# Coefficient pass spread away from the last pair, two down buffers and four sign slots, context stage with takes and squares in front of the combinations

## The chip, the core and the metric

The kernel runs on one core of a Trainium2 chip. The metric is the device time of one execution in microseconds (us). TensorE (PE) multiplies matrices from SBUF into PSUM, VectorE (DVE), ScalarE (ACT) and GpSimd (POOL) work elementwise, and the queues of SyncE (SP) and POOL issue the DMA transfers, which all run on the same 16 DMA engines. The engines run side by side; each works through its own instructions in order and waits on semaphores.

## The reference

It is one decoder layer over 2 x 512 tokens of width 1024, in three parts, each with a residual and a layer norm in front:

```
x = x + mamba2 block with its own gated MLP (gate, up, down; inner width 3584)      # first feed-forward
q1 = fake_quant(layernorm(x));  q2 = fake_quant(ctx)      # ctx 2 x 1024 x 1024
x = x + q1 @ q2                                           # context stage
W = base + mean(|w - base|) * sign(w - base)   for w1, w2, w3   # coefficient and signs
x = x + (silu(n @ W1.T) * (n @ W3.T)) @ W2.T,  n = layernorm(x)  # second feed-forward
```

`mean(|w - base|)` is one number for each of the three matrices, over 3584 x 1024 weights, so all weights must be read before the first formed weight can be written.

## The kernel before

**The two feed-forwards** (m = 0 and m = 1) are computed with a scheme of seven products in place of eight for a 2 x 2 split of each operand (`t` = 0 to 6), and each fp32 factor is split into a high and a low part, so that a product is three matmuls per tile. A *step* is 12 matmuls of 128x512 (L912 for gate and up, `product`; L937 for the down projection, `down_step`). The gate and up part has 14 *pairs* (p = 0 to 13) of 14 steps, or *turns* (7 products, each for gate, x = 0, and up, x = 1); the down part has 98 steps (2 halves `sc`, 7 products, 7 inner tiles k). Weights go through a ring of seven slots: ACT writes the high part (`weight_hi`, L1155), DVE the sum where there is one and the low part (`weight_sum`, `weight_lo` L1568), both five to six steps ahead of TensorE. The results of the gate and up steps leave PSUM by `gate_up_out` on DVE (L1654, L1664, L1674, L1682), `gate_out` (L1218 the last) and `psum_copy` on ACT. ACT and DVE go through one list of steps each and do at turn i of a pair what tables put there.

**The coefficient pass** runs beside the first feed-forward. Its 84 blocks of 128x1024 stand at the turns of `CF_TURNS` from pair 1 on: SP loads both blocks (`load_coeff`, two of 512 KB, L466) when the block two before has been used, DVE subtracts (`coeff_diff`, L1704), ACT writes the sign as int8 and sums the absolute values (`coeff_abs`), POOL stores the signs. From pair 6 on, two context tiles per pair are quantized too (`quantize`, L1708 to L1712, and `q2_sum`, at turns 5 and 9). Before: 7 blocks in each of pairs 1 to 6, 6 in each later one, 6 in pair 13.

**The last pair** of either feed-forward is where SP starts to load the down part: after turns 1, 3, ..., 13 it issues eight loads of 256 KB (`first_down_loads`, L487), 56 in all, into combination tiles that TensorE has done with, then four x quarters of 1 MB (`load_x_quarter`). SP's queue is one list; a wait in it holds up all that stands behind.

**The second feed-forward** forms its weights as it goes: `form_weight` (DVE, L1728) adds sign x coefficient to the base weights in place. Signs come through `sign_in` (2 slots), down weights through one buffer `down_formed`: SP loads (`load_down`, L597), DVE forms, POOL stores to HBM (`store_down`, L677); the next load waits for that store. The 28 down tiles are formed two in each of pairs 1 to 12 (turns 2 and 10) and four in pair 13 (turns 0, 3, 6, 9).

**The context stage** stands between. For batch b: centre, squares, variance sums on TensorE (`ctx_var`, L962), root (ACT L1399/L1400, DVE `ctx_rsqrt` L2019 to L2022), rounding of q1 (DVE and ACT in turn, `ctx_round`, ACT L1409 writes q1), products (`ctx_first`: four output tiles together, k outermost, L968, and the row sums L981; then `second_tile` one by one), a correction (`minus_mean`, L973), and `ctx_take` (DVE L2054), which adds the product to x. `ctx_columns` (ACT L1415) adds a column term to x in front of the takes, from `column_sums` (TensorE L954). `second_mean` (L986 and DVE L2047) keeps the mean of the new x. Then squares of the new x, their variance sums (three groups: rsqrt 3, 4, 5), and the combinations `comb(1, t)` (DVE L1609 makes, ACT L1201 high part, L1618/L1615 low part) that feed the second feed-forward. `prefill` fills the ring for its first steps.

## Time and profile before

| | us |
|---|---|
| three runs, median (lowest, highest) | 2228.65 (2228.29, 2229.97) |
| the profiled execution: its own time | 2227.82 |
| its span in the profile | 2226.0 |
| PE busy in the span | 2125.9 (96%) |
| DVE busy | 1667.7 (75%) |
| ACT busy | 1050.2 (47%) |

All times further down are counted from the start of the span. Up to about 363 us runs the mamba2 part, up to 455 us its output projection, from about 490 to 1308 the first feed-forward, to about 1391 the context stage, then the second feed-forward to 2221. A busy PE is not a PE at its peak: matmuls overlap, and the granted clock (PEclk, as a share of full speed) falls after TensorE has been idle.

### The profile page before, as it was taken

The page shows a single profiled execution, that of the slowest core. Times are in us where ns is not written, and L with a number is a line of the kernel's source. Part 1 is how long each engine was busy: PE and PEld are TensorE (multiplying, and loading weights), DVE is VectorE, ACT ScalarE, POOL GpSimd, SP SyncE. Part 2 cuts the span into 40 slices and gives each one's busy share as a digit, 9 for nine tenths or more (in the row PEclk, how much of TensorE's full clock was granted, in tenths as well). Part 3 has the DMA queues.
Part 4 walks back from the last instruction along what each step waited for, and adds up shares of the span by engine and source line. Part 5 has one row for each costly group of instructions (what it writes and reads, how often), then busy time and mean ns, then how long its engine had stood idle before and what let it go on. Part 6 is the DMA issues. An engine that isn't in the chain of part 4 may idle for free.

```text
span 2226.0 us, 26830 instructions
## 1 busy us (share of the span) xinstructions
PE 2125.9 (96%) x9266; PEld 1688.9 (76%) x9266; DVE 1667.7 (75%) x2498; ACT 1050.2 (47%) x1710; POOL 175.5 (8%) x287
## 2 busy tenths in 40 slices
PE   7999998969999999998999998899999999899999
PEld 4777776847888888886888853688888888788887
DVE  7776556478777888886979888977777677498785
ACT  4333234236777777775444456433333333344442
POOL 0000010000111111110000000200000000000000
PEclk9999999979999999999999998899999999999999
DMA  3151002516888989889160032644444443754201
GB/s 119 38 198 38 20 28 97 144 19 218 293 308 300 328 314 309 315 304 396 62 212 1 1 133 86 165 148 168 148 168 150 173 147 142 265 206 162 99 19 57
DMA packets 132958, 361.61 MB, mean 162 GB/s; under 512 B 16288, under 2 KB 27168, under 8 KB 129184
## 3 DMA queue, kind: packets, MB, share of 16 engines
q1 hardware_dynamic: 108912, 279.78, 36.5%
q0 software_dynamic: 23920, 80.23, 10.5%
q8 instruction: 70, 1.15, 0.2%
q14 instruction: 56, 0.46, 0.1%
HBM read 279.73 MB, written 84.41 MB: 164 GB/s over the span
## 4 chain that ended last, share of the span: by engine, by line
PE 81%; DVE 11%; ACT 3%; DMA 2%; issue 2%; SPq 1%; DVEq 0%; ACTq 0%
PE pair L912 41%; PE pair L937 24%; PE pair L717 9%; DVE conv_out L1867 1%; DVE comb_lo L1618 1%; PE pair L968 1%; SPq L487 1%; DMA down_formed<-b_dn 1%; PE pair L855 1%; PE pair L856 1%; PE pair L830 1%; DVE ring_lo L1568 1%; PE pair L837 1%; DMA wd_spill<-down_formed 1%; PE pair L753 1%
## 5 line engine op out<-in xcount | busy, mean ns | idle before, releaser
L912 PE MATMUL pair<-comb_hi,ring_hi 128*128 128x512 f32 x1568 | 618.4, 394 | 47.1 <-DVE comb_lo L1615 11.1
L912 PE MATMUL pair<-comb_lo,ring_hi 128*128 128x512 f32 x1568 | 616.0, 393 | 0.0
L912 PE MATMUL pair<-comb_hi,ring_lo 128*128 128x512 f32 x1568 | 615.4, 393 | 0.0
L912 PEld LDWEIGHTS pair<-comb_hi,ring_hi 128*128 128x128 f32 x1568 | 298.1, 190 | 117.0 <-issue 36.0
L937 PE MATMUL pair<-inner_ring_a,ring_hi 128*128 128x512 f32 x1120 | 346.4, 390 | 2.2 <-DVE second_copy_a L1674 2.2
L912 PEld LDWEIGHTS pair<-comb_hi,ring_lo 128*128 128x128 f32 x1568 | 297.9, 190 | 62.9
L912 PEld LDWEIGHTS pair<-comb_lo,ring_hi 128*128 128x128 f32 x1568 | 298.0, 190 | 61.9 <-issue 0.2
L937 PEld LDWEIGHTS pair<-inner_ring_a,ring_hi 128*128 128x128 f32 x1120 | 210.8, 188 | 46.5 <-issue 2.6
L937 PE MATMUL pair<-inner_ring_a,ring_lo 128*128 128x512 f32 x560 | 218.5, 390 | 0.0
L1155 ACT ACTIVATE ring_hi<-ring_sum 128x512 fp32r<-128x512 f32 x168 | 106.0, 631 | 157.7 <-DVE ring_sum L1555 155.8
L717 PE MATMUL pair<-act_hi,weights_hi 128*128 128x512 f32 x416 | 138.6, 415 | 12.0 <-DVE act_lo L1511 7.6
L937 PE MATMUL pair<-inner_ring_b,ring_hi 128*128 128x512 f32 x448 | 138.4, 390 | 0.0
L1568 DVE TENSOR_TENSOR ring_lo<-raw_a,ring_hi 128x512 fp32r<-128x512 f32 x140 | 95.4, 685 | 50.2 <-ACT ring_hi L1155 50.1
L717 PE MATMUL pair<-act_lo,weights_hi 128*128 128x512 f32 x416 | 129.7, 393 | 0.0
L717 PE MATMUL pair<-act_hi,weights_lo 128*128 128x512 f32 x416 | 129.3, 392 | 0.0
L1256 ACT ACTIVATE sign_out<-pair 128x1024 int8<-128x1024 f32 x84 | 85.9, 1022 | 86.7 <-DVE pair L1704 86.7
L937 PEld LDWEIGHTS pair<-inner_ring_a,ring_lo 128*128 128x128 f32 x560 | 105.5, 188 | 22.0
L1568 DVE TENSOR_TENSOR ring_lo<-ring_sum,ring_hi 128x512 fp32r<-128x512 f32 x168 | 114.9, 684 | 1.3
L1704 DVE TENSOR_TENSOR pair<-coeff_in 128x1024 f32<-128x1024 f32 x84 | 103.0, 1226 | 16.2 <-DMA coeff_in<-b_dn 14.5
L717 PEld LDWEIGHTS pair<-act_hi,weights_hi 128*128 128x128 f32 x416 | 78.0, 191 | 35.9 <-issue 20.7
L937 PEld LDWEIGHTS pair<-inner_ring_b,ring_hi 128*128 128x128 f32 x448 | 84.1, 188 | 17.9 <-issue 0.5
L717 PEld LDWEIGHTS pair<-act_lo,weights_hi 128*128 128x128 f32 x416 | 78.9, 190 | 17.0
(334 smaller groups left out, 3189.6 us busy)
## 6 DMA issues: line engine op xcount, KB each, us to landing
coeff_in<-f_gu SPq DMA_DIRECT2D x56, 512.0 KB, 5.1
coeff_in<-b_gu SPq DMA_DIRECT2D x56, 512.0 KB, 6.9
weights_raw<-w_mamba SPq DMA_DIRECT2D x28, 512.0 KB, 3.2
raw_a<-w_gu SPq DMA_DIRECT2D x28, 512.0 KB, 7.2
raw_a<-w_gu SPq DMA_DIRECT2D x56, 256.0 KB, 6.2
u_spill<-gate_a POOLq DMA_DIRECT2D x56, 256.0 KB, 6.1
coeff_in<-f_dn SPq DMA_DIRECT2D x28, 512.0 KB, 4.8
coeff_in<-b_dn SPq DMA_DIRECT2D x28, 512.0 KB, 6.8
```

The source lines that it names most:

```text
L487: sp.dma_start(d_tile(m, kind, k), src).then_inc(s_ld[group // 2][k], 16)
L717: ins = pe.matmul(out[:, half * 512:(half + 1) * 512], w[:, wi, wcol * P:(wcol + 1) * P], a[:, half * 512:(half + 1) * 512], start=first a ...
L753: return pe.matmul(out[:, HALF[b]], ones[:, :], src[:, HALF[b]], start=first, stop=last)
L830: ins = pe.matmul(ps[1][:, g * 512:(g + 1) * 512], ones[:, :], cs_rhs[:, g * HPG:(g + 1) * HPG, :], start=True, stop=False, skip_group_che ...
L837: pe.matmul(ps[2][:, g * 512:(g + 1) * 512], bx_cur[:, 2 + g, :], xbc[:, 4 + g * HPG:4 + (g + 1) * HPG, bass.ds(b * SEQ + c * P, P)], star ...
L855: pe.matmul(ps[2][:, h * P:(h + 1) * P], x_dt[:, h, :], att[:, h, :], start=True, stop=False)
L912: ins = pe.matmul(out, wt[:, slot, col], a, start=t in (0, 1, 3) and kk == 0 and n == 0, stop=kk == KH - 1 and n == 2, skip_group_check=True)
L937: ins = pe.matmul(out, wt[:, slot, col], a, start=t in (0, 1, 3) and k == 0 and n == 0, stop=k == SC_PAIRS - 1 and n == 2, skip_group_chec ...
L1155: act.activation(WRH[:, slot, :], src, ACT.Copy).then_inc(s_whi, 1)
L1256: act.activation(sign_out[:, c % 2, :], dif_ps[:, :], ACT.Sign).then_inc(s_sign, 1)
L1568: TT(WRL[:, slot, :], src, WRH[:, slot, :].bitcast(F32), ALU.subtract).then_inc(s_wlo, 1)
L1704: TT(dif_ps[:, :], dif[:, c % 2, 0, :], dif[:, c % 2, 1, :], ALU.subtract).then_inc(s_cd, 1)
```

## The change

1. `CF_TURNS`: 7 blocks in pairs 1 to 9, 6 in pairs 10 to 12, 3 in pair 13 (turns 1, 3, 6). The number of blocks is the same, 84.
2. `stage_d` becomes two buffers, used in turn by down tile; `load_down(j)` waits for the store of tile j - 2. `sign_in` becomes four slots; the signs are loaded four forms ahead. In the context stage the signs of forms 4 to 7 are loaded behind both loads of `raw_odd`.
3. Context stage: the column sums of batch 1 go behind the first products of batch 0; ACT takes the root of batch 1 between two halves of the column additions; `ctx_first` leaves its fourth output tile out up to k = `late` and makes it up behind a wait, so that batch 1's products wait for the fourth take and not for the fifth and `second_mean(0)`; both `second_mean` stand behind the last variance sums; on DVE all takes and squares of batch 1 come in front of `comb(1, 0)`.
4. Semaphores are merged (`var_ready` into `norm_var_ready`, the dt and cs ones), with the counts to match.

Core of the diff:

```diff
-CF_TURNS = {p: ((1, 3, 5, 7, 9, 11, 13) if p <= 6 else (1, 3, 6, 8, 11, 13)) for p in range(1, PAIRS)}
-CF_TURNS[PAIRS - 1] = (1, 3, 6, 7, 8, 11)
+CF_TURNS = {p: (1, 3, 5, 7, 9, 11, 13) if p <= 9 else (1, 3, 6, 8, 11, 13) for p in range(1, PAIRS)}
+CF_TURNS[PAIRS - 1] = (1, 3, 6)
...
-    stage_d = at("down_formed", 144 * KB, [P, BLK], F32)
-    sign_in = at("sign_in", 192 * KB, [P, 2, BLK], I8)
+    stage_d = (at("down_formed_a", 144 * KB, [P, BLK], F32), at("down_formed_b", 194 * KB, [P, BLK], F32))
+    sign_ab, sign_cd = at("sign_in_ab", 192 * KB, [P, 2, BLK], I8), at("sign_in_cd", 198 * KB, [P, 2, BLK], I8)
+    sign_in = (sign_ab[:, 0, :], sign_ab[:, 1, :], sign_cd[:, 0, :], sign_cd[:, 1, :])
...
         def load_down(j):
-            if j >= 1:
-                sp.wait_ge(s_do_st, 16 * j)
-            sp.dma_start(stage_d[:, :], b_dn[j]).then_inc(s_sd, 16)
+            if j >= 2:
+                sp.wait_ge(s_do_st[j % 2], 16 * (j // 2))
+            sp.dma_start(stage_d[j % 2][:, :], b_dn[j]).then_inc(s_sd[j % 2], 16)
...
         spill_x2(0)
-        load_sign(4)
-        load_sign(5)
         spill_x2(1)
         load_second(1, 0)
         load_second(1, 1)
+        for f in range(4, 8):
+            load_sign(f)
...
-        def ctx_first(b, banks, rows):
+        def ctx_first(b, banks, rows, late, start):
             for k in range(KT):
                 pe.wait_ge(s_q1, b * KT + k + 1)
-                for o in range(KH):
+                for o in range(KH if k > late else KH - 1):
                     ctx_mm(b, o, k, banks[o])
...
+                if k == late:
+                    start()
+                    for kk in range(k + 1):
+                        ctx_mm(b, KH - 1, kk, banks[KH - 1])
...
-        second_mean(0, bank(5))
-        pe.wait_ge(s_xt, 5)
-        pe.wait_ge(s_m2, 1)
-        ctx_first(1, [bank(n) for n in (1, 2, 6, 4)], bank(5))
+        pe.wait_ge(s_xt, 4)
+        ctx_first(1, [bank(n) for n in (1, 2, 6, 4)], bank(5), 2, lambda: pe.wait_ge(s_xt, 5))
...
-        ctx_columns(0, range(KT))
+        ctx_columns(0, range(KH))
         ctx_root(3, bank(7))
+        ctx_columns(0, range(KH, KT))
...
-        ctx_take(1, range(2), (1, 2))
-        prefill(1, range(2, RING))
-        ctx_take(1, range(2, KH), (6, 4))
+        ctx_take(1, range(KH), (1, 2, 6, 4))
+        ctx_take(1, range(KH, 6), (3, 0))
+        prefill(1, range(2, 4))
+        ctx_take(1, range(6, KT), (1, 2))
+        square_pairs(5, x_square, range(3))
         comb(1, 0)
-        ctx_take(1, range(KH, 6), (3, 0))
-        square_pairs(5, x_square, range(2))
-        ctx_take(1, range(6, KT), (1, 2))
-        square_pairs(5, x_square, range(2, 3))
-        second_mean(1)
-        for kk in range(KH):
-            make(1, "b21", kk)
+        second_mean(0, bank(6))
+        second_mean(1, bank(3))
         ctx_rsqrt(5, bank(7))
-        comb(1, 1, made=True)
+        comb(1, 1)
+        prefill(1, range(4, RING))
```

SP's queue in the last pair of the first feed-forward, before (`coeff_in` are the two blocks of the coefficient pass, `comb_*_f_0t` the down quarters of tile t, `ctx_in` a context tile):

```order
L487 DMA comb_lo_f_00_109<-u_spill 128x512
L466 DMA coeff_in<-f_dn 128x1024
L466 DMA coeff_in<-b_dn 128x1024
L487 DMA comb_lo_f_01_110<-w_dn 128x512
...
L487 DMA comb_lo_f_02_111<-u_spill 128x512
L466 DMA coeff_in<-f_dn 128x1024
L466 DMA coeff_in<-b_dn 128x1024
L466 DMA coeff_in<-f_dn 128x1024
L466 DMA coeff_in<-b_dn 128x1024
L487 DMA comb_lo_f_03_112<-w_dn 128x512 x4
```

and now, in the same place:

```order
L467 DMA coeff_in<-f_dn 128x1024
L467 DMA coeff_in<-b_dn 128x1024
L488 DMA comb_hi_f_00_81<-w_dn 128x512
...
L488 DMA comb_lo_f_00_109<-u_spill 128x512
L488 DMA comb_lo_f_01_110<-w_dn 128x512
...
L488 DMA comb_lo_f_02_111<-u_spill 128x512
L488 DMA comb_lo_f_03_112<-w_dn 128x512 x4
```

Three pairs of block loads are gone from between the down quarters; the last one stands in front of them.

DVE in the context stage, from the last root but one to the combinations for t = 2, before (`centred<-pair` are takes, `x_mid<-x_mid` sums of squares, `comb_hi_f_16` and `comb_lo_f_16` the makes of t = 0 and 1):

```order
L2054 SCALAR_TENSOR_TENSOR centred<-pair,quant_columns,centred 128x512 x2
L1609 TENSOR_TENSOR comb_hi_f_16_94<-centred,scratch_c_155 128x512 x2
...
L2054 SCALAR_TENSOR_TENSOR centred<-pair,quant_columns,centred 128x512 x2
L2013 TENSOR_TENSOR x_mid<-x_mid 128x512
L2047 SCALAR_TENSOR_TENSOR scratch_c_155<-pair,quant_columns,scratch_c_155 128x512
L1609 TENSOR_TENSOR comb_lo_f_16_122<-centred,scratch_c_155 128x512 x4
L2019 SCALAR_TENSOR_TENSOR scratch_c_155<-scratch_c_155 128x512
L2020 SCALAR_TENSOR_TENSOR scratch_c_155<-pair,scratch_c_155 128x512
L2022 SCALAR_TENSOR_TENSOR scratch_c_155<-scratch_c_155 128x512
L1618 TENSOR_TENSOR comb_lo_103<-comb_lo_f_16_122,comb_hi_75 128x512 x4
L1609 TENSOR_TENSOR comb_lo_f_15_121<-centred,scratch_c_155 128x512 x4
```

and now:

```order
L2060 SCALAR_TENSOR_TENSOR centred<-pair,quant_columns,centred 128x512 x2
L2019 TENSOR_TENSOR x_mid<-x_mid 128x512 x3
L1615 TENSOR_TENSOR comb_hi_f_16_94<-centred,scratch_c_157 128x512 x2
...
L2053 SCALAR_TENSOR_TENSOR scratch_c_157<-pair,quant_columns,scratch_c_157 128x512 x2
L2025 SCALAR_TENSOR_TENSOR scratch_c_157<-scratch_c_157 128x512
L2026 SCALAR_TENSOR_TENSOR scratch_c_157<-pair,scratch_c_157 128x512
L2028 SCALAR_TENSOR_TENSOR scratch_c_157<-scratch_c_157 128x512
L1615 TENSOR_TENSOR comb_lo_f_16_122<-centred,scratch_c_157 128x512 x2
...
L1574 TENSOR_TENSOR ring_lo<-raw_even,ring_hi 128x512 x3
L1615 TENSOR_TENSOR comb_lo_f_15_121<-centred,scratch_c_157 128x512 x4
```

The last takes and all three sums of squares stand in front of the first combination, the root between the two combinations, and three fills of the ring behind both.

## Rows read from the trace of the kernel before

**Rows 1.** The page, part 1: busy time, share, instructions per engine.

```profile
PE 2125.9 (96%) x9266; PEld 1688.9 (76%) x9266; DVE 1667.7 (75%) x2498; ACT 1050.2 (47%) x1710; POOL 175.5 (8%) x287
```

**Rows 2.** TensorE's waits: line, releaser, us in total, times, longest.

```profile
PE pair L912 <- DVE first_copy_b L1664: 8.4, 1, 8.4
PE pair L912 <- DVE gate_a L1664: 7.2, 1, 7.2
PE pair L962 <- DVE x_mid L2013: 6.2, 1, 6.2
```

**Rows 3.** Chain of waits, second feed-forward's last pair: start us, us, what.

```profile
1923.76 5.38 DMA wd_spill<-down_formed
...
1934.23 7.55 DMA wd_spill<-down_formed
1941.80 5.34 DMA down_formed<-b_dn
...
1954.11 266.60 PE pair L937 x1176
```

**Rows 4.** DVE timeline, both last pairs: start, us, line, operation [idle before, releaser].

```profile
993.50 0.69 DVE L1654 TENSOR_TENSOR gate_a<-first_copy_a,pair 128x512 f32<-128x512 f32 x1 [1.46 <-PE pair L912]
...
1023.12 1.23 DVE L1704 TENSOR_TENSOR pair<-coeff_in 128x1024 f32<-128x1024 f32 x1 [14.50 <-DMA coeff_in<-b_dn]
...
1913.71 0.69 DVE L1654 TENSOR_TENSOR gate_b<-first_copy_b,pair 128x512 f32<-128x512 f32 x1 [1.46 <-PE pair L912]
```

**Rows 5.** Chain of waits, first feed-forward's last pair and end.

```profile
1011.97 11.12 DMA coeff_in<-b_dn
...
1034.53 257.56 PE pair L937 x1128
...
1307.81 3.19 PE pair L954 x128
```

**Rows 6.** Windows: stretch, us, busy per engine, granted clock, DMA share, GB/s.

```profile
718.70:756.80 38.10, 37.67 (x167) 30.90 (x166) 30.50 (x45) 29.11 (x49) 6.97 (x13) 1.00 0.94 326
756.80:794.90 38.10, 38.10 (x170) 31.55 (x169) 31.94 (x46) 27.75 (x47) 6.95 (x12) 1.00 0.91 323
996.00:1057.00 61.00, 51.54 (x213) 41.76 (x212) 42.05 (x65) 33.84 (x58) 5.92 (x11) 0.92 1.05 396
1911.00:1958.00 47.00, 38.58 (x162) 31.47 (x161) 23.66 (x36) 15.17 (x28) 3.53 (x7) 0.89 0.95 344
```

**Rows 7.** TensorE timeline, context stage.

```profile
1311.96 5.14 PE L1008 MATMUL pair<-x_mid,ones_over_dm 128*128 128x512 f32 x8
...
1343.59 1.88 PE L986 MATMUL pair<-x_mid_rounded,x_mid 4*128 4x512 f32 x4
1348.79 1.87 PE L968 MATMUL pair<-q,q 128*128 128x512 bf16 x4 [3.32 <-DVE centred L2054]
...
1360.76 3.70 PE L962 MATMUL pair<-x_mid,ones_over_dm 128*128 128x512 f32 x8
```

**Rows 8.** DVE timeline, context stage: the last three roots, first make for t = 2.

```profile
1334.57 0.69 DVE L2019 SCALAR_TENSOR_TENSOR scratch_c<-scratch_c 128x512 f32<-128x512 f32 x1 [3.64 <-ACT scratch_c L1400]
...
1365.88 0.69 DVE L2019 SCALAR_TENSOR_TENSOR scratch_c<-scratch_c 128x512 f32<-128x512 f32 x1 [3.72 <-ACT scratch_c L1400]
...
1393.05 0.69 DVE L2019 SCALAR_TENSOR_TENSOR scratch_c<-scratch_c 128x512 f32<-128x512 f32 x1 [3.52 <-ACT scratch_c L1400]
...
1397.64 3.09 DVE L1609 TENSOR_TENSOR comb_lo_f<-centred,scratch_c 128x512 f32<-128x512 f32 x5
```

**Rows 9.** TensorE's waits in the stretch 740 to 760 us.

```profile
PE pair L912 <- ACT gate_a L1218: 0.4, 1, 0.4
```

**Rows 10.** ACT timeline, context stage.

```profile
1328.31 4.99 ACT L1415 ACTIVATE centred<-centred,column_terms 128x512 f32<-128x512 f32 x8
1333.21 0.66 ACT L1399 ACTIVATE scratch_c<-pair,quant_columns 128x512 f32<-128x512 f32 x1
...
1350.01 0.71 ACT L1409 ACTIVATE q<-scratch_c,quant_columns 128x512 bf16<-128x512 f32 x1
```

More of the change, by code:

```diff
@@ L357, in build @@
     s_sq, s_sqd = sem("square_ready"), sem("square_used")
-    s_t, s_root = sem("var_ready"), sem("root_ready")
     s_a, s_ah, s_act = sem("act_value"), sem("act_hi_ready"), sem("act_ready")
@@ L389, in build @@
     s_q2 = [sem(f"q2_in{b}") for b in range(BATCH)]
-    s_sgn = [sem(f"sign_in{i}") for i in range(2)]
+    s_sgn = [sem(f"sign_in{i}") for i in range(4)]
     s_sign, s_form = sem("sign_ready"), sem("second_formed")
     s_so = [sem(f"sign_stored{i}") for i in range(2)]
-    s_sd, s_do_st = sem("down_raw_in"), sem("down_formed_stored")
+    s_sd = [sem(f"down_raw_in{i}") for i in range(2)]
+    s_do_st = [sem(f"down_formed_stored{i}") for i in range(2)]
     s_x1, s_u2, s_c5 = sem("first_copied"), sem("second_copied"), sem("fifth_copied")
@@ L601, in _ @@
         load_second(0, 0)
-        load_sign(0)
-        load_sign(1)
+        for f in range(4):
+            load_sign(f)
         load_second(0, 1)
-        load_sign(2)
-        load_sign(3)
         load_down(0)
+        load_down(1)
         def spill_x2(b):
@@ L625, in _ @@
                     f = FORM_AT[14 * p + turn - 1]
-                    if f + 2 < N_FORM:
-                        load_sign(f + 2)
+                    if f + 4 < N_FORM:
+                        load_sign(f + 4)
                 if 14 * p + turn - 2 in FORM_AT:
                     what = FORM_WHAT[FORM_AT[14 * p + turn - 2]]
-                    if what[0] == "d" and what[1] + 1 < ITILES:
-                        load_down(what[1] + 1)
+                    if what[0] == "d" and what[1] + 2 < ITILES:
+                        load_down(what[1] + 2)
                 if p == PAIRS - 1:
@@ L813, in _ @@
         pe.matmul(ps[2][:, 256:320], tri, a_all[:, :, :], start=True, stop=True)
[L814 removed]
+        pe.matmul(ps[2][:, 320:384], ones[:, :], a_all[:, :, :], start=True, stop=True).then_inc(s_dtm, 1)
         conv_pair(CONV_TILES // 2 - 1)
@@ L997, in _ @@
         feed_forward(W_END[0] - 2, W_END[0])
-        for b in range(BATCH):
-            column_sums(b, bank(3))
+        column_sums(0, bank(3))
         pe.wait_ge(s_xs, 2)
@@ L1012, in _ @@
         pe.wait_ge(s_m1, 1)
-        pe.wait_ge(s_ht, 3)
+        pe.wait_ge(s_ht, 2 + BATCH + 1)
         pe.wait_ge(s_q2[0], 16 * KT)
-        pe.wait_ge(s_do, 4 * 13 + KH)
-        ctx_first(0, [bank(n) for n in (0, 1, 2, 6)], bank(5))
+        ctx_first(0, [bank(n) for n in (0, 1, 2, 6)], bank(5), 0, lambda: pe.wait_ge(s_do, 4 * 13 + KH))
+        column_sums(1, bank(3))
         ctx_var(bank(7), x_square, range(KH), KT + KH, (), 0)
@@ L1064, in _ @@
         minus_mean(1, bank(2))
-        second_mean(1, bank(5))
-        pe.wait_ge(s_ht, 5)
+        pe.wait_ge(s_ht, 4 + BATCH + 1)
         ctx_var(bank(7), x_square, range(3), KT + 3 * KH, (6, 7), 5 * KT)
-        pe.wait_ge(s_xt, 2 * KT)
-        feed_forward(BASE_G[1], BASE_G[1] + 1)
+        second_mean(0, bank(6))
+        second_mean(1, bank(3))
+        feed_forward(BASE_G[1], BASE_G[1] + 4)
         pe.wait_ge(s_m2, 2)
-        feed_forward(BASE_G[1] + 1, W_END[1])
+        feed_forward(BASE_G[1] + 4, W_END[1])
     @blk.scalar
@@ L1188, in inner_hi @@
                         act.wait_ge(s_so[i], 16 * (CF_BLOCKS // 2))
-                if m == 1 and slot == 4:
-                    act.wait_ge(s_do_st, 16 * ITILES)
+                if m == 1 and slot >= 4:
+                    for i in range(2):
+                        act.wait_ge(s_do_st[i], 16 * (ITILES // 2))
                 if m == 1 and slot >= 5:
@@ L1447, in _ @@
         ctx_root(4, bank(7))
-        for w in range(2, RING):
+        ctx_columns(1, range(KH, KT))
+        for w in range(2, 4):
             weight_hi(BASE_G[1] + w)
-        ctx_columns(1, range(KH, KT))
-        taken_squares(1, range(KH))
+        taken_squares(1, range(KT))
         comb_hi(1, 0)
-        taken_squares(1, range(KH, KT))
+        ctx_root(5, bank(7))
         comb_hi(1, 1)
-        ctx_root(5, bank(7))
+        for w in range(4, RING):
+            weight_hi(BASE_G[1] + w)
         feed_forward(1)
@@ L1716, in form_tile @@
             if what[0] == "d":
-                return stage_d[:, :]
+                return stage_d[what[1] % 2][:, :]
             return rawF[what[1] % 2][:, what[2], 2 * what[3]:2 * what[3] + 2, :].rearrange("p a h -> p (a h)")
@@ L2041, in rows_lo, with second_mean @@
             STT(mean_rows(b, 1), bank(5)[0:4, :], -1.0 / DM, mean_rows(b, 0).bitcast(F32), ALU.mult, ALU.subtract).then_inc(s_rlo, 1)
-        def second_mean(b):
+        def second_mean(b, out):
             kept = scr_c(7)[:, HALF[b]]
@@ L2046, in second_mean @@
             dve.wait_ge(s_csumd, b + 2)
-            STT(kept, bank(5), S12, kept, ALU.mult, ALU.add).then_inc(s_m2, 1)
+            STT(kept, out, S12, kept, ALU.mult, ALU.add).then_inc(s_m2, 1)
         def ctx_take(b, tiles, banks):
@@ L2079, in _ @@
         ctx_take(0, range(6, KT), (3, 0))
-        second_mean(0)
         ctx_round(1, range(6, KT + 1))
```

47 lines of the change are left out of this document (25 added, 22 removed).

## The prediction

> **What bounds the kernel now.** I read the page's busy times first: TensorE is busy for 2125.9 of 2226.0 us [rows 1]. The rest of the time, and the time that its matmuls lose to a lower granted clock, are all that this change can reach. The list of TensorE's waits says where it stands still: 8.4 us for `first_copy_b`, 7.2 us for `gate_a`, 6.2 us for the sums of squares of L2013 [rows 2]. The waits of the first two blocks of the kernel (L717, L753) are longer in sum but lie outside the change.
>
> Step length: 1176 matmuls take 266.60 us [rows 3], so a step of 12 matmuls takes 2.72 us and a pair of 14 steps 38.08 us.
>
> *First feed-forward, last pair.* The DVE row of L1654 at 993.50 [rows 4] comes at the end of step 2, so this pair began at 993.50 - 3 x 2.72 = 985.3 and its 14 steps should end at 1023.4. The down steps (L937) begin at 1034.53 [rows 5], 11.1 us late. Their first 1128 matmuls then take 257.56 us where 94 steps need 255.7, 1.9 us more, the slow restart after the idle time. Together 13.0 us. The cause is the DVE row at 1023.12: it stood 14.5 us for block 82 of the coefficient pass, whose load was issued at 1011.97 and took 11.12 us [rows 4, 5]. SP had issued it behind the down quarters, and the DMA engines were full: 396 GB/s from 996 to 1057 [rows 6].
>
> *Second feed-forward, last pair.* L1654 at 1913.71 [rows 4] puts the pair's start at 1905.55 and its end at 1943.6; the down steps begin at 1954.11, 10.5 us late [rows 3]. The chain of waits goes store, load, form, store, load through the one buffer `down_formed`: 5.38 us of store, 7.55 us of store, 5.34 us of load [rows 3]. The steps at turns 3, 6 and 9 come every 8.16 us, and one round of store and load takes 12.9 us (7.55 + 5.34).
>
> *Context stage.* TensorE waits 3.3 us before the second batch's products start at 1348.79 [rows 7], and 6.2 us before the last group of variance sums [rows 2]. Behind that the limit is VectorE: the combinations for t = 2 of the second feed-forward start at 1397.64 [rows 8], and TensorE waits for them and for the ring several times before it has caught up.
>
> **The change part by part.** The sum is made against the profiled execution's own 2227.82 us; the median of the runs is 0.8 us above.
>
> 1. *Last pair of the first feed-forward: -13.0 us.* Blocks per pair fall from 6 to 3; only block 83 is still loaded in it, in front of the down quarters. Of the four block loads that stood in this queue one is left, 3.1 MB (3 x 2 x 0.52) less. Is there another wait right behind? SP issues 8 quarters (2.1 MB) after each second step. From 996 on: 1.2 MB of backlog (my estimate from the 3.1 MB issued in the 6 us before), 12.6 MB of quarters, 0.5 of context, 4.2 MB of x quarters, 2 MB of stores: 20.5 MB, or 52 us at 396 GB/s, to 1048. In that order the set of turn 5, with the inner tiles of k = 1 to 4, is in by about 1012 (first needed 1012.5 by ACT, five steps ahead of TensorE); the set of turn 11 by 1030 (needed by VectorE from 1026.1, by TensorE from 1042); the first x quarter by 1038.6 (needed at 1042.4). So everything is in before TensorE wants it, with the 13 us of the seven-slot ring to spare. Bounds: 7.9 (only the 3.1 MB leave, at 396 GB/s) to 13.0.
>
> 2. *Pairs 7 to 9: +1.3 us.* Each gets one block more (DVE 1.23 us, ACT 2.1 us) beside its two context tiles. Pair 6 already has just this load: DMA share 0.94 and TensorE busy 37.67 of 38.10 us [rows 6], with one wait of 0.4 us for ACT's `gate_a` [rows 9]. Pair 7, with one block less, has none (38.10 busy). 3 x 0.43 = 1.3. Bounds 0 to 4 (if a late pair hands its lateness on).
>
> 3. *Last pair of the second feed-forward: -10.5 us.* With two buffers the load of tile 26 goes out where that of tile 25 went (about 1915.7), is in at about 1922 and is wanted at turn 6, 1905.55 + 16.3 + 1 = 1923. Tile 27 waits for the store of tile 25 (formed 1915.5, stored by 1922 to 1924), and is in by about 1928 to 1930, wanted at turn 9, 1931. The last store ends near 1941, when ACT wants inner slot 4, five steps before TensorE. VectorE may stand for up to 3 us at turn 11 and after, because the same bytes now have to come in 10 us less; the ring covers it. Bounds: 5 to 10.5. The four sign slots change nothing by themselves: before, no wait of TensorE lies in pairs 1 to 12. In pair 0 the signs of forms 4 to 7 now stand in SP's queue behind both `raw_odd` loads (2.1 MB), which the forms need anyway.
>
> 4. *Context stage: -6.5 us.* (a) Half of the column sums (3.19 us together, [rows 5]) goes behind the first products: these start 1.6 us earlier, less what the clock takes (L1008 needs 5.14 us behind the column sums, L962 with as many matmuls 3.70, [rows 7]). (b) ACT takes 4 of the 8 column additions (4.99 us, [rows 10]) behind the root of L1399, so the root starts when the variance sums end, 1331 to 1333.3, not at 1333.21 [rows 10]; I take 1332, 1.2 us earlier. The chain behind (L2019 at 1334.57, takes, rounding) moves by as much. (c) The second batch's products no longer wait for `second_mean(0)` (0.7 us on DVE, 1.9 us on PE) nor for the fifth take, but for the fourth, with the fourth bank caught up at k = 2. TensorE had no other work from 1343.6 on than L986 [rows 7], so the products start there or soon after; the pace is then the rounding: the column for k = 4 was written from 1350.01 on [rows 10] and is ready 1.9 us earlier (1.2 from (b), 0.7 from `second_mean(0)`), 1348.9; TensorE is at 1349.1 by then, and four steps of 1.28 us and the rest of the fourth end at 1354.2 where it was 1360.8 [rows 7]: 6.6 us. Lower end of the gain 5, upper 7.5 (root at 1331.3). (d) From the variance sums to the root L1399 and L2019 (1365.88 before, [rows 8]) the order is as before, so VectorE goes on 6.3 us earlier. (e) Behind it the same operations stand in another order: eight takes, three sums of squares, two combinations of eight operations, two mean updates (one more than before), the root, nine prefill operations. Before, from 1368.1 (1365.88 and three operations) to 1397.64 it took 29.6 us, of them 3.5 us idle in front of L2019 at 1393.05 [rows 8]. Now the squares are ready in front of the first combination, so the root is computed beside it; but each combination alternates with ACT at its own pace (1 us lost each, as the first one does now), and the takes of tiles 4 to 7 wait for TensorE (0.5 us at each of two places). I come to 29.2 us: 0.4 us gained. 6.3 + 0.4 = 6.7, taken as 6.5. (f) Behind 1397.64 VectorE works without a gap until TensorE has caught up, before and after, with the same instructions, so what it gains in front is what the kernel gains. Bounds 0 (see rival B) to 8.
>
> 5. *Merged semaphores* (`var_ready` into `norm_var_ready` and so on): counts only, 0.
>
> Sum: -13.0 + 1.3 - 10.5 - 6.5 = -28.7; 2227.8 - 28.7 = 2199.1, by the runs' median 2200.
>
> On the DMA rate: the row shows 396 GB/s over 61 us, reads and stores together [rows 6].
> The Trainium skill (DMA: Bandwidth & Descriptors, Specifications and Where 436 GB/s comes from) gives an HBM limit of about 358 GB/s per core when both cores of a pair stream, and 425 measured for one core alone; by the 358 the 20.5 MB of part 1 would take 57 us and the first x quarter would come at about 1043, just when it is wanted. The trace of this one-core program is above the 358, so I stay with 396.
>
> **Rivals.**
>
> A. *The DMA engines are the true limit of both last pairs.* Then removing DVE's wait only moves it to the quarter loads. For it: the share of 1.05 over 61 us [rows 6], and that the same quarters must now arrive 10 to 13 us sooner. Against it: before, TensorE has no wait in either down phase, and the ring is five steps ahead. Price: the first stage gets back 3.1 MB / 0.396 = 7.9 us, the second what 344 instead of 396 GB/s left over 47 us [rows 6], 47 x (1 - 344/396) = 6.2. Sum: -7.9 + 1.3 - 6.2 - 6.5 = -19.3: 2209. The same time would come if the waits fell away and most of the clock's loss stayed.
>
> B. *The context stage gives nothing.* If the part behind L2019 is longer by what the part before is shorter (two combinations in a row, each in step with ACT, and two mean updates on VectorE in front of the last root), or the start of the products at the fourth take runs into the rounding, 6.5 us go: 2206.5. Speaks for it: VectorE has hardly an idle stretch there but those in front of L2019. Against: the 6.6 us of (c) lie in front of a VectorE that idles 3.7 us before 1365.88 [rows 8], at the end of a chain that starts with TensorE.
>
> C. *Slower: pairs 7 to 9 tip over.* The mechanism is that of 1023 in three more places: a block's load comes late, VectorE stands with it in order, and `gate_a` and the ring behind it are late for TensorE. One such wait cost 13 us; three of them are 39 us against the 30 that the other parts give: 2227.8 + 39 - 30 = 2237. It decides once the blocks cost more than 10 us per pair, that is, when a load lands over 10 us late. Against it: pair 6 with the same bytes loses 0.43 us.
>
> D. *The change does not do what it says in the second feed-forward:* tile 27 still waits for the store of tile 25, that store took 7.55 us at its worst, and the load comes behind two sets of quarters; if it lands at 1938 instead of 1930, VectorE stands 7 us and TensorE perhaps 2: 2202. Small, inside the range.
>
> **How the numbers follow.** My forecast with its small variants (and D) 0.68, A 0.15, B 0.10, C 0.03, and 0.04 for something not seen here that eats nearly all of it (0.01 still faster, 0.02 the same, 0.01 slower). The likeliest is 2200. A and B together would be 2216, too unlikely to be held. The range goes from 2195 (no cost in pairs 7 to 9, 8 us in the context stage, a little more clock) to 2212 (A with a little of B). About 0.2% (4.5 us) is what a measurement can tell from no change. So faster 0.94, same 0.02, slower 0.04.
>
> **What would show it right or wrong.** In the profile after: no wait of VectorE over 1 us on `coeff_in` and on `down_formed`; L937 begins 38.1 us after the last pair's start in both halves (within 1 us); three more waits of about 0.4 us on `gate_a` L1218 at the ends of pairs 7 to 9; the second batch's products start without a wait near the end of the first batch's and end 6 to 7 us earlier, counted from the end of the first feed-forward; the first combination for t = 2 starts 6 to 7 us earlier by the same count. I am wrong if L937 shows gaps in its first fourteen steps with DMA behind them (A), if the distance from L2019 to the t = 2 combinations has grown (B), or if pairs 7 to 9 are longer than 39 us (C).

## The result and the profile after

| | before | after |
|---|---|---|
| median of the runs (lowest, highest), us | 2228.47 (2228.20, 2229.97), 4 runs | 2204.30 (2200.11, 2204.72), 4 runs |
| ratio, 95% interval | | 0.9886 (0.9869 to 0.9903) |
| profiled execution: own time, span | 2227.82, 2226.0 | 2204.26, 2202.4 |

The change takes 24 us off; 2200 was predicted. The line numbers have moved by a few: L912 is now L913, L937 L938, L962 L963, L1218 L1222, L1704 L1710.

First TensorE's busy time, part 1 of the page, which answers to [rows 1], and the list of its waits (line, releaser, us in total, times, longest):

```profile
PE 2123.8 (96%) x9262; PEld 1687.1 (77%) x9266; DVE 1668.0 (76%) x2498; ACT 1051.5 (48%) x1710; POOL 174.8 (8%) x287
```

```profile
PE pair L913 <- DVE comb_lo L1621: 12.4, 6, 6.0
...
PE pair L913 <- ACT gate_a L1222: 2.6, 5, 0.8
PE pair L963 <- DVE x_mid L2019: 1.8, 1, 1.8
```

The waits of 8.4 us for `first_copy_b` and 7.2 for `gate_a` L1664 [rows 2] are gone, and the 6.2 us for the sums of squares are 1.8. What has grown is small: there are five waits for `gate_a` L1222 (2.6 us) where the trace of before has two (0.9 us, one of them in [rows 9]). The three more stand at the ends of pairs 7 to 9 and are the price of the blocks there. The six waits for `comb_lo` L1621 at the starts of the feed-forwards are 12.4 us in place of 11.1, the longest 6.0 in place of 3.3.

The chain of waits of the changed kernel, start, us, what:

```profile
530.09 209.74 PE pair L913 x924
...
876.08 152.56 PE pair L913 x672
1028.64 255.69 PE pair L938 x1128
...
1930.54 266.57 PE pair L938 x1176
```

In both halves the products of the last pair run straight into the down steps. The 1128 matmuls take 255.69 us, which is 94 of the steps of 2.72 us, so nothing is lost to a lower clock, where [rows 5] had 257.56. The two down phases begin at 1028.64 and 1930.54, where [rows 5] and [rows 3] have 1034.53 and 1954.11.

To see where the 23.6 us of span went, I cut both profiled executions at the first and the last matmul of each kind (views of the product line and of the down line: first and last start):

| stretch | before | after | difference |
|---|---|---|---|
| start to the first product of the first feed-forward | 471.7 | 474.4 | +2.7 |
| first feed-forward, products and down | 835.7 | 825.3 | -10.4 |
| context stage and the second feed-forward's products | 646.6 | 630.7 | -15.9 |
| second down phase and end | 272.0 | 272.0 | 0.0 |

The first row is not the change's; e4 and e10 deal with it. How far such stretches differ between executions of the same code stands in the last section.

### The profile page after: what moved, and what is told of

Its sections match the earlier page's. It is cut to its first block, busy times and chain, and to the rows that moved or that the text cites. A ratio compares the mean times of both kernels' runs of the same rounds, so it can differ in the third digit from the quotient of the medians.

```text
span 2202.4 us, 26828 instructions
## 1 busy us (share of the span) xinstructions
PE 2123.8 (96%) x9262; PEld 1687.1 (77%) x9266; DVE 1668.0 (76%) x2498; ACT 1051.5 (48%) x1710; POOL 174.8 (8%) x287
## 4 chain that ended last, share of the span: by engine, by line
PE 82%; DVE 12%; ACT 3%; issue 2%; DMA 1%; DVEq 0%; SPq 0%; ACTq 0%
PE pair L913 41%; PE pair L938 24%; PE pair L718 9%; DVE conv_out L1873 1%; PE pair L969 1%; DVE comb_lo L1624 1%; DVE ring_lo L1574 1%; PE pair L831 1%; DVE pair L1710 1%; PE pair L856 1%; PE pair L857 1%; PE pair L838 1%; PE pair L754 1%; PE pair L860 1%; PE pair L963 1%
## 5 line engine op out<-in xcount | busy, mean ns | idle before, releaser
L913 PE MATMUL pair<-comb_hi,ring_hi 128*128 128x512 f32 x1568 | 618.4, 394 | 34.7 <-DVE comb_lo L1621 12.4
L913 PE MATMUL pair<-comb_hi,ring_lo 128*128 128x512 f32 x1568 | 615.6, 393 | 0.0
L913 PE MATMUL pair<-comb_lo,ring_hi 128*128 128x512 f32 x1568 | 615.6, 393 | 0.0
L913 PEld LDWEIGHTS pair<-comb_hi,ring_hi 128*128 128x128 f32 x1568 | 297.8, 190 | 106.8 <-issue 22.9
L913 PEld LDWEIGHTS pair<-comb_hi,ring_lo 128*128 128x128 f32 x1568 | 297.7, 190 | 62.5
L913 PEld LDWEIGHTS pair<-comb_lo,ring_hi 128*128 128x128 f32 x1568 | 298.2, 190 | 61.5
L938 PE MATMUL pair<-inner_ring_a,ring_hi 128*128 128x512 f32 x1120 | 344.9, 389 | 0.0
L938 PEld LDWEIGHTS pair<-inner_ring_a,ring_hi 128*128 128x128 f32 x1120 | 210.1, 188 | 43.6
L938 PE MATMUL pair<-inner_ring_a,ring_lo 128*128 128x512 f32 x560 | 217.9, 389 | 0.0
L938 PE MATMUL pair<-inner_ring_b,ring_hi 128*128 128x512 f32 x448 | 138.3, 390 | 0.0
L938 PEld LDWEIGHTS pair<-inner_ring_a,ring_lo 128*128 128x128 f32 x560 | 105.1, 188 | 21.9
L1710 DVE TENSOR_TENSOR pair<-coeff_in 128x1024 f32<-128x1024 f32 x84 | 103.0, 1227 | 0.3 <-DMA coeff_in<-b_gu 0.3
L938 PEld LDWEIGHTS pair<-inner_ring_b,ring_hi 128*128 128x128 f32 x448 | 84.1, 188 | 17.9 <-issue 0.5
```

What stands on the lines that cost most here:

```text
L913: ins = pe.matmul(out, wt[:, slot, col], a, start=t in (0, 1, 3) and kk == 0 and n == 0, stop=kk == KH - 1 and n == 2, skip_group_check=True)
L938: ins = pe.matmul(out, wt[:, slot, col], a, start=t in (0, 1, 3) and k == 0 and n == 0, stop=k == SC_PAIRS - 1 and n == 2, skip_group_chec ...
L1710: TT(dif_ps[:, :], dif[:, c % 2, 0, :], dif[:, c % 2, 1, :], ALU.subtract).then_inc(s_cd, 1)
```

## The experiments

All medians are of four or more runs; the kernel before gave 2224.2 to 2234.8 in 50 runs beside them, and I take a median of five as good to about 1.5 us. Where less matters I go by the stretches of the traces. Line numbers of the variants differ by a few from those of the changed kernel.

### e1: the block table alone

```diff
-CF_TURNS = {p: ((1, 3, 5, 7, 9, 11, 13) if p <= 6 else ...
-CF_TURNS[PAIRS - 1] = (1, 3, 6, 7, 8, 11)
+CF_TURNS = {p: (1, 3, 5, 7, 9, 11, 13) if p <= 9 else ...
+CF_TURNS[PAIRS - 1] = (1, 3, 6)
```

> Only CF_TURNS changed (7 blocks in pairs 1 to 9, 6 in 10 to 12, 3 in pair 13). Theory 1 (the parts act by themselves, as the two traces read): the last pair gives 13.0 us back, pairs 7 to 9 cost 2.6 us (their lengths in the trace after are 38.8, 39.2 and 38.8 us for 38.1), net -10.4: 2218.1 us. Theory 2 (the 2.8 us that the changed kernel is later before its first feed-forward belong to this part): 2220.9. The prediction's own numbers: -13.0 + 1.3 = -11.7, 2216.8. Rival A (DMA engines are the limit): about -5, 2223.

Measured 2220.25 us (2218.38 to 2221.09) against 2228.1; ratio 0.9963 (0.9949 to 0.9977), so -7.9 us. In its trace the first feed-forward takes 825.5 us, 10.2 less than in the trace of before, as theory 1 says. But the kernel before does not always lose so much there: in e2, e4 and e8, which have its block table, the same stretch takes 833.9, 834.1 and 833.6 us (in e3, which has it too, 835.3). So the table, gain in the last pair less cost in pairs 7 to 9, is worth 8.1 to 10.4 us by the executions that one compares. With the 2.6 us that pairs 7 to 9 cost, the last pair gives back 10.7 to 13.0 us, and the 13.0 that the prediction read from one trace are the upper end. Rival A's 5 us stands at the very edge of the interval (0.9977) and above all five runs; the trace speaks against it with its 10.2 us.

### e2: buffers and sign slots; e8: the sign slots alone; e4: the merged semaphores alone

e2 has `stage_d` and `sign_in` as in the change, without the other parts; e8 is e2 with

```diff
-    stage_d = (at("down_formed_a", ...), at("down_formed_b", ...))
+    stage_d = (at("down_formed", 144 * KB, [P, BLK], F32),) * 2
...
-            if j >= 2:
-                sp.wait_ge(s_do_st[j % 2], 16 * (j // 2))
+            if j >= 1:
+                sp.wait_ge(s_do_st[(j - 1) % 2], 16 * ((j - 1) // 2 + 1))
```

and `load_down(j + 1)` for `load_down(j + 2)`. Both need the merged semaphores, which e4 has alone.

> Only the two down buffers and the four sign slots, with the merged semaphores (there are none left for the new ones otherwise). Theory 1: -10.5 us, 2218.0. Theory 2 (the merged semaphores cost the 2.8 us before the first feed-forward): -7.7, 2220.8. Rival A (the down quarters' loads are the true limit of the last pair): -4.3, 2224.2.

> As e2_buffers, but with one down buffer and four sign slots. Theory 1 (the sign slots do nothing by themselves): 2228.5, with the second last pair's lateness of about 10 us back, against 2218.6 with both. Theory 2 (the signs, loaded four ahead, are half of it): 2223.

> Only the merged semaphores. Theory 1 (the head of the program varies by itself from build to build or run to run): 2228.5, within 1 us. Theory 2 (the merge costs the 2.8 us): 2231.3.

| | median (range), us | ratio (95%) |
|---|---|---|
| e2 | 2218.61 (2217.14 to 2220.58) | 0.9958 (0.9944 to 0.9972) |
| e8 | 2228.23 (2227.00 to 2229.91) | 1.0002 (0.9994 to 1.0011) |
| e4 | 2228.68 (2227.86 to 2230.36) | 1.0006 (0.9997 to 1.0015) |

Four sign slots with one down buffer give nothing, so e2's 9.5 us need the second down buffer. (Two buffers with two sign slots were not run.) VectorE's waits for the down weights in the last pair of the second feed-forward, of e8 and then of the changed kernel, and with them one of the changed kernel for a down quarter:

```profile
DVE down_formed L1729 <- DMA down_formed<-b_dn: 21.3, 3, 10.3
```

```profile
DVE down_formed_a L1734 <- DMA down_formed_a<-b_dn: 2.7, 1, 2.7
...
DVE down_formed_b L1734 <- DMA down_formed_b<-b_dn: 0.9, 1, 0.9
```

```profile
DVE comb_lo_f L1553 <- DMA comb_hi_f<-u_spill: 6.8, 1, 6.8
```

The round of store and load held VectorE for 21.3 us in three waits; with two buffers 3.6 are left. A wait of 6.8 us for a down quarter has come in their place; the trace of before has none, that of e2 one of 7.3. The ring hides all of these from TensorE, which goes from the products into 266.57 us of down steps without a wait, as the chain above shows. The merge of the semaphores costs nothing that 11 runs can tell: theory 2 of e4 falls, and with it any tie of the +2.7 us to the change, which has no other edit in front of the first feed-forward.

### e3: the context stage alone

The edits of part 3 of the change, with the semaphores as before.

> Only the context stage's part, semaphores as before. Theory 1 (as the two traces read, from the end of the first feed-forward to the start of the second's products): -5.3 us, 2223.2. The prediction's number: -6.5, 2222.0. Rival B: 0, 2228.5. If part of the gain in the changed kernel comes from the signs and the down buffer being loaded in another order, it is less than 5 here.

Measured 2222.09 us (2220.67 to 2224.15, 9 runs) against 2228.1; ratio 0.9974 (0.9964 to 0.9984), so -6.0. Rival B, which gave the context stage nothing, is out. The three parts give -7.9, -9.5 and -6.0 by themselves, -23.4 together; the change gave -24.2. They add up within what medians of five can tell: none eats a visible part of another's gain.

### e5: the last root in front of the kept means

In the changed kernel VectorE's rows from the end of `comb(1, 0)` on (start, us, line, operation, idle before and its releaser):

```profile
1371.71 0.75 DVE L2053 SCALAR_TENSOR_TENSOR scratch_c<-pair,quant_columns,scratch_c 128x512 f32<-128x512 f32 x1 [2.00 <-PE pair L992]
1373.43 0.75 DVE L2053 SCALAR_TENSOR_TENSOR scratch_c<-pair,quant_columns,scratch_c 128x512 f32<-128x512 f32 x1 [0.97 <-PE pair L992]
1374.09 0.68 DVE L2025 SCALAR_TENSOR_TENSOR scratch_c<-scratch_c 128x512 f32<-128x512 f32 x1
...
1381.45 1.29 DVE L1556 TENSOR_TENSOR raw_even<-raw_even 128x512 f32<-128x512 f32 x2
```

The root L2025 has been ready since 1371.1, when ACT's L1404 (1370.45, 0.63 us) ended, but both `second_mean` stand in front of it and wait 3.0 us for TensorE's L992. e5 puts the two ring sums (L1556) and the root there first:

```diff
+        for n in range(4, RING):
+            if step_of(BASE_G[1] + n)[3] in SUMMED:
+                weight_sum(BASE_G[1] + n)
+        ctx_rsqrt(5, bank(7))
         second_mean(0, bank(6))
         second_mean(1, bank(3))
-        ctx_rsqrt(5, bank(7))
         comb(1, 1)
-        prefill(1, range(4, RING))
+        for n in range(4, RING):
+            weight_lo(BASE_G[1] + n)
```

> The changed kernel, with VectorE's part behind comb(1, 0) in another order: the two sums of the ring's slots 4 and 5 first, then the last root, then both second_mean, then comb(1, 1) and the low parts. In the trace after, VectorE stands 2.0 and 1.0 us for TensorE's L992 before both second_mean, with the root behind them, and starts the makes for t = 2 at 1384.65. Theory 1 (these waits are what the context stage fell short by, and TensorE waits for this chain): the makes start 2.8 us earlier and the kernel with them, 2201.5. Theory 2 (the ring or TensorE's own order binds there): 2204.3, no change.

Its rows in the same place:

```profile
1365.79 1.29 DVE L1556 TENSOR_TENSOR raw_even<-raw_even 128x512 f32<-128x512 f32 x2
1367.28 0.69 DVE L2025 SCALAR_TENSOR_TENSOR scratch_c<-scratch_c 128x512 f32<-128x512 f32 x1 [0.20 <-ACT scratch_c L1404]
...
1369.45 1.41 DVE L2053 SCALAR_TENSOR_TENSOR scratch_c<-pair,quant_columns,scratch_c 128x512 f32<-128x512 f32 x2
...
1377.77 3.09 DVE L1615 TENSOR_TENSOR comb_lo_f<-centred,scratch_c 128x512 f32<-128x512 f32 x5
```

The waits are 0.2 us in all, and from the last operation of `comb(1, 0)` to the makes for t = 2 it is 13.4 us where it was 16.4: the 3.0 us. TensorE gets about half of them. Context stage and products take 627.6 us for 630.7, but 1.5 of these 3.1 us lie at the start of the stage, in front of the edit: there e7 and e9, which have the changed kernel's context stage, are as early as e5, and their stretch takes 629.2 us. Against them e5 is 1.6 us shorter. At its third wait for `comb_lo` TensorE is still 3.1 us earlier than theirs (counted from the end of the first feed-forward); then it waits 5.6 us for ACT's `second_copy_b` where they wait 3.8 us for the ring. The median, 2203.84 (2198.83 to 2204.80), is only 0.5 us under the changed kernel's, whose own runs reach from 2200.07 to 2205.81: by the times alone this run decides nothing; e12 has the same order again.

### e6, e7, e9: what pairs 6 to 9 cost

Each edits `CF_TURNS` in the changed kernel: e6 to eight blocks in pairs 1 to 5 (turns 1, 3, 5, 6, 8, 10, 11, 13), six in 6 to 12, two in 13; e7 to turns 1, 3, 4, 6, 8, 11, 13 in pairs 6 to 9; e9 to 1, 3, 5, 7, 8, 10, 13 there.

> The changed kernel with 8 coefficient blocks in each of pairs 1 to 5 (turns 1, 3, 5, 6, 8, 10, 11, 13), 6 in pairs 6 to 12 and 2 in pair 13. Theory 1 (seven blocks beside two context tiles are what makes pairs 6 to 9 0.7 to 1.1 us too long, and pairs 1 to 5 have room because they quantize no context tile): pairs 6 to 9 take 38.1 us each, 3.3 us less, 2201.0. Theory 2 (eight blocks cost TensorE in pairs 1 to 5 what they cost in pairs 6 to 9, 0.7 us each): 2204.5.

> The changed kernel with seven blocks in pairs 6 to 9 as before, but at turns 1, 3, 4, 6, 8, 11, 13, so that none shares its turn with a context tile (turns 5 and 9). Theory 1 (the amount of work per pair makes the wait): still 38.8 us per pair, 2204.3. Theory 2 (block and context tile in one turn make VectorE and ACT late at the end of the pair): pairs of 38.1 us, 2201.0.

> The changed kernel with the seven blocks of pairs 6 to 9 at turns 1, 3, 5, 7, 8, 10, 13. In the trace after, the wait at the end of these pairs is a chain: VectorE's difference of the block of turn 11 starts 33.8 us after the pair's start (32.3 with six blocks), ACT needs 2.2 us for its sign and sum, then writes one ring slot and only then takes gate_a (L1222) out of PSUM, for which TensorE waits. Theory 1 (the place of that block decides): with the block at turn 10 gate_a is in time, the pairs take 38.1 us, 2204.3 - 3.3 = 2201.0. Theory 2 (the amount of work decides): the pairs stay at 38.8 us or more, 2204.3 or above.

| | median (range), us | first feed-forward's products, us |
|---|---|---|
| changed kernel | 2204.30 | 553.9 |
| e6 | 2207.46 (2204.84 to 2208.77) | 557.3 |
| e7 | 2202.24 (2201.62 to 2203.76) | 556.0 |
| e9 | 2205.34 (2204.26 to 2205.74) | 555.5 |

None is better in that stretch. (e7's lower median does not come from there, as far as its one trace shows: the first product starts at 472.3 us instead of 474.4, and the context stage is 1.5 us shorter, with the same code.) Both theories of e6 miss: pairs 6 to 9 take the 38.1 us of theory 1, but pairs 2 to 5 cost more than the 0.7 us each of theory 2. e6 by windows of a pair each, pairs 2, 3, 4 and then 6 and 7 (us, busy per engine, granted clock, DMA share, GB/s):

```profile
568.40:607.60 39.20, 38.35 (x168) 31.46 (x168) 28.53 (x40) 29.05 (x48) 6.46 (x12) 1.00 0.92 319
607.60:647.50 39.90, 38.32 (x168) 31.46 (x168) 29.77 (x42) 30.18 (x51) 6.47 (x12) 1.00 0.91 317
647.50:687.30 39.80, 38.36 (x168) 31.45 (x168) 29.10 (x41) 29.65 (x49) 6.47 (x12) 1.00 0.91 315
...
726.90:765.00 38.10, 38.06 (x168) 31.55 (x169) 31.91 (x46) 28.15 (x47) 6.95 (x12) 1.00 0.91 324
765.00:803.10 38.10, 38.10 (x170) 31.56 (x169) 31.12 (x45) 27.70 (x46) 6.96 (x12) 1.00 0.89 310
```

Six blocks beside two context tiles cost nothing (38.1), eight blocks without a tile 1.1 to 1.8 us, although VectorE is less busy there (28.5 to 29.8 us against 31.9). So VectorE's share of busy time is not the limit. What TensorE waits for stands in ACT's rows at the end of pair 7 of the changed kernel:

```profile
794.75 1.02 ACT L1260 ACTIVATE sign_out<-pair 128x1024 int8<-128x1024 f32 x1 [1.19 <-DVE pair L1710]
795.80 1.01 ACT L1263 ACTIVATE pair<-pair 128x1024 f32<-128x1024 f32 x1
...
796.82 0.62 ACT L1158 ACTIVATE ring_hi<-raw_a 128x512 fp32r<-128x512 f32 x1
797.34 0.59 ACT L1222 ACTIVATE gate_a<-pair 128x512 f32<-128x512 f32 x1
```

and TensorE's first product behind it:

```profile
798.07 0.47 PE L913 MATMUL pair<-comb_hi,ring_hi 128*128 128x512 f32 x1 [0.43 <-ACT gate_a L1222]
```

TensorE wants the bank that L1222 empties. In front of L1222 ACT takes the sign and the sum of the block of turn 11 (2.1 us), for which it idles 1.19 us until VectorE has made the difference. Pair 7 began at 759.28; VectorE's difference starts 34.2 us later (793.49). In the trace of before it began at 756.48 and the difference came at 789.06, 32.6 us later, and L1218 was in time (792.90). So VectorE comes to this block 1.6 us later in a pair that has one more in front of it, whose difference takes 1.23 us. That this block makes the 1.6 us is an argument from the rows; no run shows it alone.

e9 moves the block of turn 11 to turn 10 and fails: VectorE waits for loads instead.

```profile
DVE pair L1712 <- DMA coeff_in<-b_gu: 5.8, 2, 3.3
DVE pair L1712 <- ACT pair L1265: 3.4, 2, 1.7
```

With blocks at turns 7 and 8 the next loads are issued close together, and a difference also waits for ACT to release the one before. Where no load was late, at the ends of pairs 6 and 9, the wait was 0.35 and 0.36 us instead of 0.43 and 0.44: moving the block gained next to nothing. e7 has the same fault (2.0 us for `coeff_in`, 1.9 for `ctx_in`) and shows a second cost:

```profile
836.14 0.47 PE L915 MATMUL pair<-comb_hi,ring_hi 128*128 128x512 f32 x1 [1.85 <-ACT gate_a L1224]
...
837.17 0.63 PE L915 MATMUL pair<-comb_lo,ring_hi 128*128 128x512 f32 x1
```

```profile
836.10:875.90 39.80, 39.76 (x168) 32.62 (x168) 32.12 (x46) 29.79 (x50) 7.64 (x13) 0.96 0.90 325
```

Behind the wait of 1.85 us, at the end of three late pairs, matmuls of 0.39 us take 0.63 for some microseconds (clock 0.96 over the pair, between its levels of 1.2 and 2.4 GHz), so the pair took 1.7 us more. After e6's waits of 1.0 to 1.4 us, and after one of 1.9 us in e9, the clock stayed at 1.00. Theory 1 of e9 and theory 2 of e7 fall; for blocks in pairs 6 to 9 evenly spaced turns (1, 3, ..., 13) are the best of those tried.

### e11: the bytes back, without the waits

```diff
+                if p == PAIRS - 1 and turn in (4, 7, 9):
+                    s = int(turn == 7)
...
+                    for i, src in enumerate((f_dn, b_dn)):
+                        sp.dma_start(dif[:, s, i, :], src[turn]).then_inc(s_cf[s], 16)
```

> The changed kernel with three more pairs of 512 KB loads in the last pair of the first feed-forward (turns 4, 7, 9), into the coefficient blocks' buffer, read by nobody: the 3.1 MB that the change takes out of this queue are back, the waits of VectorE are not. Theory 1 (what cost 13 us was VectorE waiting for a block behind the down quarters, not the bytes): 2204.3, at most 1 us more. Rival A (the DMA engines are the limit): 3.1 MB / 0.396 = 7.9 us more, 2212.

Measured 2208.77 us (2206.16 to 2209.14), 4.5 above the changed kernel beside it (e10). Both theories miss: the bytes are not free and not worth 7.9. In the stretch of the down phase VectorE waits for a down quarter, and TensorE now for VectorE, of e11 and then of the changed kernel:

```profile
DVE comb_lo_f L1562 <- DMA comb_hi_f<-u_spill: 9.2, 1, 9.2
```

```profile
PE pair L947 <- DVE inner_ring_b L1614: 2.0, 1, 2.0
```

```profile
DVE comb_lo_f L1553 <- DMA comb_hi_f<-u_spill: 5.7, 1, 5.7
```

The changed kernel has that wait already, 5.7 us, and the trace of before has none there: the DMA engines have come next in line, and the ring of seven slots hides them. 3.1 MB more make it 9.2 us, and the down steps take 275.3 us instead of 271.2: 2.0 of wait and the slow matmuls behind it (granted clock 0.91 from 1040 to 1060 us). So the bytes were 4.5 of the 10.7 to 13.0 us; the rest was lost because VectorE, which works in order, stood 14.5 us for a block that came behind the down quarters. Two things stay open. Whether the same six blocks would do with their loads in front of the quarters, no run shows. And e11 has the bytes of before, but not their places: its last pair of loads goes out at 1023.8, 32.6 us after the pair's start, where before it was 27.1. Either way the bytes are close to being a limit of their own.

### e10: the changed kernel again

> The changed kernel as it is, again. Its four times were 2200.11 to 2204.72, and in the traces so far the first product of the first feed-forward starts at 471.7 to 475.7 us whatever was changed. If that scatter is of the execution and not of the kernel, the median is 2203 to 2205 again with single runs as low as 2200.

2204.29 us (2200.07 to 2205.81). The first product of the first feed-forward started, in the profiled executions, at 471.7 us (before), 474.4 (after), 473.6 to 475.7 (e1 to e4), 475.0 here and 472.3 to 475.1 in the others. The kernel before, e1 and e3 do not differ in front of it even by a semaphore, and e1 and e3 are 1.9 and 3.3 us later. It is a scatter of executions, and the profiled execution of before was the earliest of all. The expectation for e10 held.

### e12: e5's order and one block in pair 0

e5's order, and one block moved from pair 9 to turn 13 of pair 0:

```diff
-CF_TURNS = {p: (1, 3, 5, 7, 9, 11, 13) if p <= 9 else ...
+CF_TURNS = {p: (1, 3, 5, 7, 9, 11, 13) if p <= 8 else ...
+CF_TURNS[0] = (13,)
```

> The changed kernel with VectorE's order of e5_means and one coefficient block moved from pair 9 to turn 13 of pair 0, so that pair 9 has six again. Theory 1: 3.0 us from the context stage (what e5_means' trace shows between the end of the first feed-forward and its last step, 627.4 against 630.5 us) and 0.7 us from pair 9 (38.1 for 38.8 us): 2204.3 - 3.7 = 2200.6. Theory 2 (e5_means' median of 2203.84 tells the truth and its trace was a lucky one): 2203. Theory 3 (pair 0 has no room, since TensorE waits there for VectorE anyway): up to 2 us worse than theory 1, 2202.6.

2201.64 us (2199.14 to 2202.93, 4 runs) against 2228.79; ratio 0.9883 (0.9866 to 0.9899). That is 2.7 us under the changed kernel's median, near theory 1, but the intervals of the two ratios overlap, so it is likely, not shown. The trace gives less: the products of the first feed-forward take 552.7 us for 553.9, with one wait for `gate_a` less, and context stage and products 628.4 for 630.7. Of the latter 2.3 us, 1.5 are again the early start of the stage; against e7 and e9 (629.2) 0.8 us are left. So the edits account for about 2 us, nearer theory 3 (2202.6) than theory 1 (2200.6).

## Why the prediction was right, and where its sizes were off

- *Bound and mechanisms.* Both last pairs, the context stage and the price in pairs 7 to 9 are where the time moved, in the predicted directions, and the parts add up. Most of the announced signs are there: L938 follows the products at once in both halves, three more waits of 0.4 to 0.8 us for L1222, no wait of VectorE over 1 us for `coeff_in`, and the second batch's products end 6.7 us earlier. Four signs went the other way. VectorE waits 2.7 us for `down_formed_a`, and 6.8 us for a down quarter in the same pair, where the text allowed 3 us; it rightly counted on the ring. Pair 8 takes 39.2 us, above the 39 set as a sign of rival C. The distance from the root to the combinations for t = 2 has grown by 1.5 us, the sign set for rival B. And these combinations start 5.2 us earlier, not 6 to 7. The last two are step (e) of part 4.
- *Part 1, -13.0.* Right against the profiled execution. As a size for the kernel it was too big, since it came from one execution: against the stretches of e2, e4 and e8 it is 1.6 to 2.1 us less, mostly because the first 1128 down matmuls, 257.56 us in [rows 5], take 255.95 in e2 and e8. So the 1.9 us of slow restart are not there in every execution. What the text priced at 7.9 us, the bytes alone, e11 measures at 4.5.
- *Part 2, +1.3.* Measured 2.6: pairs 7, 8 and 9 take 38.8, 39.2 and 38.8 us for 38.1. I had counted the wait in the list (0.43) and not what the trace shows beside it: in such a pair the busy time also holds 38.35 us for 38.08, so each costs 0.7 us and more.
- *Part 3, -10.5.* Right: 10.5 in the traces, 9.5 by e2's median; e8 shows that there is none of it without the second buffer.
- *Part 4, -6.5.* In the traces 5.2, by e3's median 6.0 (e3's own trace has 6.7, with the early start of the stage in it). Steps (a) to (d) held: the second batch's variance sums start at 1346.33, 6.7 us earlier when counted from the end of the first feed-forward (which came 7.8 us earlier), for 6.6 predicted. Step (e) failed: from the end of the root to the makes for t = 2 it takes 31.1 us (1353.56 to 1384.65) where I said 29.2 and where before it took 29.6. I had named the two `second_mean` in front of the root and not priced what they wait for: 3.0 us for TensorE's L992. Rival B had named these mean updates, and it was right to that extent. e5 takes the two waits away; VectorE's chain is 3.0 us shorter and TensorE gets 1.6 of them. So step (f), by which TensorE gains what VectorE gains, holds for the change (5.2 us of either) and not beyond it.
- *Rival A* (2209) has more in it than I gave it: no part of it reached TensorE, but VectorE waits 5.7 and 6.8 us for down quarters in the two last pairs where before it waited for none, and e11 shows that the limit begins within 3.1 MB of the changed kernel. From 1010 to 1050 us the DMA engines of the changed kernel are as full as in [rows 6], by the last two columns of the windows below (DMA share, GB/s). The Trainium skill (DMA: Bandwidth & Descriptors, Measured) gives about 358 GB/s per core when both cores of a pair stream; this one-core program is above it in that stretch of either trace.

```profile
1010.00:1022.00 12.00, 12.00 (x55) 9.93 (x54) 8.11 (x13) 8.54 (x15) 1.62 (x3) 1.00 1.05 395
...
1034.00:1050.00 16.00, 16.00 (x72) 13.25 (x71) 13.63 (x23) 6.93 (x12) 0.00 (x0) 1.00 1.05 389
```

- *Rival C* (2237): with seven evenly spaced blocks the worst load came 0.3 us late for VectorE (0.5 us in e10). It took 10.06 us from issue to landing (814.95 to 825.03), in pair 8, the one of 39.2 us; so the margin there is thin. e7 and e9 show the first step of it, with uneven ones: 1.9 us of waits at a pair's end and, once, the clock.
- *The sum.* 2199.1 was predicted for the profiled execution and it took 2204.26. The 5.2 us are 2.7 in front of the first feed-forward (scatter), 1.3 in pairs 7 to 9 and 1.3 in the context stage. In medians the gain is 24.2 us for 28.7, and the misses all go one way: 1.6 to 2.1 us in the last pair of the first feed-forward, 1.3 in pairs 7 to 9, 1.3 in the context stage.

## What to carry to other kernels

When work is taken off a stretch that a queue of loads feeds, ask first which engine, working in order, waits for a load that stands late in the queue, and only then for the bytes: with VectorE waiting for them the three pairs of loads cost 10.7 to 13.0 us here, with nobody waiting the same bytes cost 4.5. A part that an engine does between two others' hand-overs is priced by the latest moment at which it can start, not by the engine's busy share. A chain that is made shorter pays the next engine only up to the next wait: 3.0 us on VectorE were 1.6 on TensorE. Before a few microseconds of a section are put down to an edit, compare the same section in executions that the edit does not touch: here they differ by 1.5 to 4 us.
